# Cross attention of a two-layer decoder: heads in steps of two pairs, with the turned probabilities packed four blocks to a PSUM bank

## The reference

```python
q = (x @ w_q).reshape(B, SQ, 16, 64)       # B = 8, SQ = 112
k = (cond @ w_k).reshape(B, SKV, 16, 64)   # SKV = 375
v = (cond @ w_v).reshape(B, SKV, 16, 64)
attn = softmax(einsum('bqhd,bkhd->bhqk', q, k) * 64 ** -0.5)
out = einsum('bhqk,bkhd->bqhd', attn, v).reshape(B, SQ, 1024)
return out @ w_out + b_out
```

## Time and profile before

| | us |
|---|---|
| three runs | 1166.77, 1177.46, 1171.46 |
| median of them | 1171.46 |
| span of the profiled execution | 1165.0 |
| stage 4's heads in it | from 661.7 to about 961 |

### The profile page before, as it was taken

One profiled execution on the slowest core, in us unless ns is written; L12 is line 12 of the kernel. 1 busy time (PEld: TensorE's weight loads), 2 busy tenths in 40 slices (PEclk: granted clock), 3 DMA queues, 4 the chain that ended last, 5 costly groups with the idle time before them and its releaser, 6 DMA issues.

```text
span 1165.0 us, 21556 instructions
## 1 busy us (share of the span) xinstructions
PE 1001.8 (86%) x8624; PEld 707.4 (61%) x8624; DVE 640.4 (55%) x1519; ACT 588.3 (50%) x1374; POOL 284.6 (24%) x292
## 2 busy tenths in 40 slices
PE   7996898887689988789998799889888897789995
PEld 4664565665388854456655676667666665447654
DVE  3246545666669833454455476776676664527003
ACT  5532565552468844344544354556555544465741
POOL 2521412100500033211112202221132124132733
PEclk9988889898989999899999988999999888679998
DMA  9341464102679785422252243313222105000001
GB/s 311 99 86 40 112 127 110 45 12 98 209 272 314 259 278 168 139 88 85 80 173 88 81 120 105 101 34 107 81 57 78 27 1 226 1 1 1 1 1 32
DMA packets 66676, 123.68 MB, mean 106 GB/s; under 512 B 11632, under 2 KB 41968, under 8 KB 62496
## 3 DMA queue, kind: packets, MB, share of 16 engines
q1 hardware_dynamic: 64528, 117.48, 33.0%
q0 software_dynamic: 2048, 4.82, 1.4%
HBM read 86.30 MB, written 35.92 MB: 105 GB/s over the span
## 4 chain that ended last, share of the span: by engine, by line
PE 56%; DVE 19%; ACT 11%; DMA 5%; issue 4%; POOL 4%; SPq 1%; another core or an unknown queue 0%; DVEq 0%; ACTq 0%; POOLq 0%
PE psum L398 38%; DVE s_p L2695 3%; ACT s_p L2653 3%; POOL rs L2985 2%; PE psum L2612 2%; DVE s_max L2684 2%; PE psum L2623 2%; PE psum L1369 2%; PE psum L2784 1%; DVE s_pT L2676 1%; PE psum L550 1%; DVE s_max L653 1%; PE psum L2173 1%; PE psum L2159 1%; PE psum L2604 1%
## 5 line engine op out<-in xcount | busy, mean ns | idle before, releaser
L2653 ACT ACTIVATE s_p<-psum,s_max 112x375 f32<-112x375 f32 x128 | 72.3, 569 | 87.6 <-DVE s_max L2684 87.6
L693 POOL TENSOR_TENSOR rstd<-meanvar,minus_half 112x1 f32<-112x1 f32 x40 | 23.1, 578 | 279.6 <-DVE meanvar L645 209.9
L653 DVE TENSOR_REDUCE s_max<-psum 112x2 f32<-112x750 f32 x64 | 59.4, 935 | 32.5 <-PE psum L550 31.4
L2985 POOL TENSOR_TENSOR rs<-ms,minus_half 112x32 f32<-112x32 f32 x8 | 43.5, 5442 | 110.3 <-DVE ms L2919 110.3
L398 PE MATMUL psum<-Wv,ctx 128*125 128x512 f16 x240 | 59.6, 392 | 11.2 <-ACT s_v L624 5.4
L398 PE MATMUL psum<-ctx,Wk 128*128 128x375 f16 x320 | 62.8, 331 | 5.0 <-ACT s_yT L2242 2.8
L2684 DVE TENSOR_REDUCE s_max<-psum 112x1 f32<-112x375 f32 x128 | 63.7, 539 | 2.3 <-PE psum L2604 2.1
L2612 PE MATMUL psum<-ident,s_p 112*125 112x112 f32 x384 | 61.4, 294 | 3.9 <-DVE s_p L2695 2.3
L609 ACT ACTIVATE s_k<-psum 128x375 f16<-128x375 f32 x64 | 31.2, 488 | 62.1 <-PE psum L398 59.5
L2604 PE MATMUL psum<-s_k,s_q 64*112 64x375 f16 x384 | 46.0, 345 | 17.0 <-ACT s_p L2653 6.5
L2612 PEld LDWEIGHTS psum<-ident,s_p 112*125 112x125 f32 x384 | 51.7, 198 | 13.7 <-DVE s_p L2695 3.9
(11 more groups left out here) (360 smaller groups left out, 2445.1 us busy)
## 6 DMA issues: line engine op xcount, KB each, us to landing
keys<-s_k SPq DMA_DIRECT2D x64, 187.5 KB, 2.2
s_k<-keys SPq DMA_DIRECT2D x8, 1500.0 KB, 7.6
values<-s_v SPq DMA_DIRECT2D x48, 224.0 KB
s_v<-values SPq DMA_DIRECT2D x16, 672.0 KB
raw_wg<-in_wg SPq DMA_DIRECT2D x8, 1024.0 KB, 6.6
raw_wu<-in_wu SPq DMA_DIRECT2D x8, 1024.0 KB, 7.1
raw_wd<-in_wd SPq DMA_DIRECT2D x8, 1024.0 KB
s_kd<-k_halves SPq DMA_DIRECT2D x48, 93.8 KB, 3.8
```

The source lines that it names most:

```text
L653: VE.tensor_reduce(s1_max[b % 2][:, 2 * p:2 * p + 2], rings["s1"][unit][0:N, :, 0:S], X, ALU.max, negate=True).then_inc(*V.up("max1", n))
L2653: SC.activation(rings["p4"][2 * n + j], rings["s4"][(n, j)][0:N, 0:S], ACT.Exp, bias=s4_max[b % 2][:, h:h + 1], accum_out=s4_sum[b % 2][:, ...
L2985: GP.tensor_tensor(rs5[b % 2][:], ms5[b % 2][:], minus_half[:], ALU.pow).then_inc(*G.up("rs5", b))
```

## The change

Two pairs go together. In step m the stream places the turning of step m-2 (two pairs, twelve blocks, four to a bank in three banks, where it was three to a bank in four), `nm4` of both pairs of step m-1, `sc4` of both pairs of step m, and `av4` of both pairs of step m-2. It yields after each of the three turned banks and after the two `av4`; from the third turned bank to the last `av4` nothing can come between. ACT copies two of the three banks, 448 columns each, DVE the third. `oT4` comes first in its step. There are eight buffers of probabilities instead of six. The planned costs of turning are three times 430 for two pairs, where they were four times 320. Scores, maxima, exps, scalings and products are as they were.

```diff
--- before.py
+++ after.py
@@ -2357,15 +2357,15 @@
         for name, shape in things:
             ffn_w[name] = group.load(ffn_m, name, shape)
             ffn_group[name] = group
+    NS, TURNED = B * HP // 2, 3
     s4_q.append(work.tensor("s4_q1", [P, HP, 2, 2 * N], F16))
     s4_k.append(work.tensor("s4_k1", [P, HP, 2, S], F16))
     s4_v.append(work.tensor("s4_v2", [SCH, NCH, H // 2, DHW]))
-    s4_p = [work.tensor(f"s4_p{i}", [N, S])[:] for i in range(6)]
-    s4_pT = [work.tensor(f"s4_pT{i}", [SCH, NCH * N])[:] for i in range(4)]
+    s4_p = [work.tensor(f"s4_p{i}", [N, S])[:] for i in range(8)]
+    s4_pT = [work.tensor(f"s4_pT{i}", [SCH, TURNED, 4, N]) for i in range(2)]
     s4_max = [work.tensor(f"s4_max{i}", [N, H]) for i in range(2)]
     s4_sum = [work.tensor(f"s4_sum{i}", [N, H]) for i in range(2)]
     assert work.at <= s3_end
-    TO_T, TO_O = 2, 3
     xf = wts.tensor("xf", [P, KC, T_])
     xf16 = wts.tensor("xf16", [P, 2, KC, T_], F16)
     k5 = [wts.tensor(f"k5_{i}", [P, KC, 2, N]) for i in range(2)]
@@ -2391,8 +2391,8 @@
     rings.update(s4=w4, t4=w4, misc4=w4, misc5=w4, o4=banks(6, 1), o5=banks(7, 1),
                  p4=Ring(s4_p), pT4=Ring(s4_pT), sc5=Ring(sc5), pT5=Ring(pT5))
     step("sc4", "T sc4, V maxa4, V maxb4, A expa4, A expb4", cost=500)
-    step("trA4", "T tr4, A pT4", "t4", "A pT4", 320)
-    step("trV4", "T tr4, V pT4", "t4", "V pT4", 320)
+    step("trA4", "T tr4, A pT4", "t4", "A pT4", 430)
+    step("trV4", "T tr4, V pT4", "t4", "V pT4", 430)
     step("nm4", "V +1, V nma4, V nmb4")
     step("av4", "T av4", cost=700)
     step("oT4", "A oT4")
@@ -2459,31 +2459,40 @@
             yield from until(("av4", 4 * (m - 3) + 3))
         yield [("vget", m)]
 
+    def turned_of(h):
+
+        return range(NCH * h // 4, (NCH * h + NCH - 1) // 4 + 1)
+
     def s4_heads():
 
-        for n in range(B * HP + TO_O + 1):
-            b, p = divmod(n, HP)
-            if n < B * HP and p == 0:
-                yield from until(("k4get", b), ("q4", 4 if b > 1 else 3, b - b % 2, HW // P - 1))
-            t, o = n - TO_T, n - TO_O
-            if 0 <= t < B * HP:
-                for h, what in ((2 * t, "trA4"), (2 * t + 1, "trV4")):
-                    rings["pT4"].take(h, (T, ("av4", t)))
-                    place((what, h))
-            if o > 0 and o % 4 == 0:
-                place(("oT4", (o - 1) // HP, (o - 1) % HP // 4))
-            if 0 < n <= B * HP:
-                place(("nm4", n - 1))
-            if n < B * HP:
-                for j, name in enumerate(("expa4", "expb4")):
-                    rings["s4"].take((n, j), (A, (name, n)))
-                    rings["p4"].take(2 * n + j, (T, ("tr4", 2 * n + j)))
-                yield [("sc4", n)]
-            if 0 <= o < B * HP:
-                if o % 4 == 0:
-                    yield from until(("vget", o // 4))
-                    rings["o4"].take(o // 4, (A, ("oT4", o // HP, o % HP // 4)))
-                yield [("av4", o)]
+        for m in range(NS + 3):
+            t = m - 2
+            if t > 0 and t % 2 == 0:
+                place(("oT4", (t - 1) // 4, (t - 1) // 2 % 2))
+            if 0 <= t < NS:
+                rings["pT4"].take(t, (T, ("av4", 2 * t + 1)))
+                for k in range(TURNED):
+                    yield [("trV4" if k == TURNED - 1 else "trA4", t, k)]
+            if 0 < m <= NS:
+                place(("nm4", 2 * m - 2))
+                place(("nm4", 2 * m - 1))
+            if m < NS and m % 4 == 0:
+                yield from until(("k4get", m // 4), ("q4", 4 if m >= 8 else 3, m // 4 - m // 4 % 2, HW // P - 1))
+            if m < NS:
+                for n in (2 * m, 2 * m + 1):
+                    for j, name in enumerate(("expa4", "expb4")):
+                        rings["s4"].take((n, j), (A, (name, n)))
+                        h = 2 * (n % 2) + j
+                        rings["p4"].take(2 * n + j, (T, ("tr4", m, turned_of(h)[-1])))
+                    if n % 2 == 0 or t >= 0:
+                        place(("sc4", n))
+                    else:
+                        yield [("sc4", n)]
+            if 0 <= t < NS:
+                if t % 2 == 0:
+                    yield from until(("vget", t // 2))
+                    rings["o4"].take(t // 2, (A, ("oT4", t // 4, t // 2 % 2)))
+                yield [("av4", 2 * t), ("av4", 2 * t + 1)]
         place(("ffnin",))
 
     def s4_out(b):
@@ -2605,24 +2614,31 @@
                                         k[rows, p, v, :], start=i == 0, stop=i == 2)
                 ins.then_inc(*T.up("sc4", n))
             elif what in ("trA4", "trV4"):
-                h, = at
-                p = rings["p4"][h]
-                pe.wait_ge(V["nmb4" if h % 2 else "nma4", h // 2], *rings["t4"].free(unit))
-                for c in range(NCH):
-                    ins = TE.transpose(rings["t4"][unit][0:SCH, c * N:(c + 1) * N],
-                                       p[:, c * SCH:(c + 1) * SCH], ident[0:N, 0:N])
-                ins.then_inc(*T.up("tr4", h))
+                t, k = at
+                for h in range(4):
+                    if k in turned_of(h):
+                        pe.wait_ge(V["nmb4" if h % 2 else "nma4", 2 * t + h // 2])
+                pe.wait_ge(*rings["t4"].free(unit))
+                for i in range(4):
+                    h, c = divmod(4 * k + i, NCH)
+                    ins = TE.transpose(rings["t4"][unit][0:SCH, i * N:(i + 1) * N],
+                                       rings["p4"][4 * t + h][:, c * SCH:(c + 1) * SCH], ident[0:N, 0:N])
+                ins.then_inc(*T.up("tr4", t, k))
             elif what == "av4":
                 n, = at
                 b, p = divmod(n, HP)
-                pe.wait_ge(A["pT4", 2 * n], V["pT4", 2 * n + 1], L_vget[n // 4 % 3]["vget", n // 4])
+                t = n // 2
+                pe.wait_ge(A["pT4", t, 1], L_vget[n // 4 % 3]["vget", n // 4])
+                if n % 2:
+                    pe.wait_ge(V["pT4", t, TURNED - 1])
                 if p % 4 == 0:
                     pe.wait_ge(*rings["o4"].free(n // 4))
                 for c in range(NCH):
                     for j in range(2):
+                        k, i = divmod(NCH * (2 * (n % 2) + j) + c, 4)
                         ins = TE.matmul(rings["o4"][n // 4][64 * j:64 * j + 64, p % 4 * N:(p % 4 + 1) * N],
                                         s4_v[n // 4 % 3][:, c, 2 * (p % 4) + j, :],
-                                        rings["pT4"][2 * n + j][:, c * N:(c + 1) * N],
+                                        rings["pT4"][t][:, k, i, :],
                                         start=c == 0, stop=c == NCH - 1)
                 ins.then_inc(*T.up("av4", n))
             elif what == "out":
@@ -2640,10 +2656,11 @@
         for unit in plans[4]:
             what, *at = unit
             if what == "trA4":
-                h, = at
-                act.wait_ge(T["tr4", h], *rings["pT4"].free(h))
-                SC.activation(rings["pT4"][h], rings["t4"][unit][0:SCH, 0:NCH * N],
-                              ACT.Copy).then_inc(*A.up("pT4", h))
+                t, k = at
+                act.wait_ge(T["tr4", t, k], *rings["pT4"].free(t))
+                SC.activation(rings["pT4"][t][:, k].rearrange("p i n -> p (i n)"),
+                              rings["t4"][unit][0:SCH, 0:4 * N],
+                              ACT.Copy).then_inc(*A.up("pT4", t, k))
             elif what == "sc4":
                 n, = at
                 b, p = divmod(n, HP)
@@ -2671,10 +2688,10 @@
         for unit in plans[4]:
             what, *at = unit
             if what == "trV4":
-                h, = at
-                dve.wait_ge(T["tr4", h], *rings["pT4"].free(h))
-                VE.tensor_copy(rings["pT4"][h],
-                               rings["t4"][unit][0:SCH, 0:NCH * N]).then_inc(*V.up("pT4", h))
+                t, k = at
+                dve.wait_ge(T["tr4", t, k], *rings["pT4"].free(t))
+                VE.tensor_copy(rings["pT4"][t][:, k].rearrange("p i n -> p (i n)"),
+                               rings["t4"][unit][0:SCH, 0:4 * N]).then_inc(*V.up("pT4", t, k))
             elif what == "sc4":
                 n, = at
                 b, p = divmod(n, HP)
```

## The result

The changed kernel takes 1184.3 us (median of 12 runs) beside 1171.7 for the kernel before: a ratio of 1.0099, with a 95% interval of 1.0066 to 1.0132. Run again beside other kernels it was 1.0068 (1.0032 to 1.0105). It is slower by 0.7 to 1%, where 0.7% faster was forecast.

The account below looks back on a forecast made before the run. TensorE was taken to set the pace, though not alone. Terms -18.8 - 4.4 - 3.0 + 17 + 1 = -8.2 us took 1171.5 to 1163 us; forecast 1155 to 1171 (chance 0.42), range 1147 to 1185.

Parts of the forecast that it names:

- What bounds the kernel: Stage 4: TensorE sets the pace, but not alone; it idles 34.1 of 299 us, partly waiting for exps and copies.
- Part 1: TensorE in stage 4: 125 fewer changes of array split at 0.15 us each, -18.8 us; lower bound 0.09 each, -11.3.
- Part 2: Products' wait for the results' copy (oT4) goes, -4.4 us; clock lost behind it in first 59 us returns, -3.0.
- Part 3: Copies of turned banks: DVE 12.4 us less, ACT 5.6 us more, both hidden by PE's work: 0.
- Part 4: Maxima behind a second scaling on DVE hold banks: 33 us of waits in 31 steps, +17 net of old waits.
- term for s5's waits: Within Part 4: half of PE's 12.2 us of waits for s5's copies and exps, 6 us, taken off the new wait.
- Short of banks: Rival, chance 0.20: steps wait 1.6 us for their second exp, clock gives nothing back, s5 waits stay: +18 us, 1189.
- Waits as they were: Rival, chance 0.22: new wait costs no more than exps did before, both clock episodes go: -28 us, 1143.
- The other half of the chain: Rival, chance 0.10: DVE and ACT hold the pace, a shorter PE list only becomes idle time: 1171, no change.
- The clock: Rival, chance 0.06: new pauses drop TensorE's clock in some eight steps with few fillers: +20 on the sum, 1183.
- What would show it: Stage 4 signs: PE busy 15 to 20 us less, s_p waits some 30, twelve turned blocks 1.5 us, early clock above 0.86.
- signs of being wrong: PE busy falls under 8 us; s_p waits stay 10 or pass 45; or stage length stays while idle replaces work.

Follow-up runs that it names:

- alternating variant: Scalings first, with the first pair's products placed between the two pairs' scores in a step: 1134.0 us, 0.9722 of the kernel before.
- scalings first: The changed kernel with both scalings (nm4) of step m-1 placed first in step m, ahead of the turned banks: 1132.0 us, 0.9716 of the kernel before.
- six copies: Scalings first, plus six DVE copies that nothing needs ahead of each step's maxima: 1203.3 us, 1.0335 of the kernel before.

## Why the prediction was wrong

**What bounds the kernel** was read rightly: PE, held up by banks. All variants move with PE's idle time and clock.

**Part 1, changes of split.** Forecast -18.8 us at 0.15 each. PE's work was 248.6 us before and is 234.8 and 235.0: -13.7, 0.11 us a change, 5 us less than forecast. The price itself is not sharp: 0.12 to 0.13 in the alternating variant, and 0.14 if the kernel before is set against scalings first, which has the changed kernel's list but 3 to 5 us less work. So the value lies between the forecast's bounds of 0.09 and 0.15, and whether the price was too high or waits added to the work is not shown.

**Part 2, the results' copy.** The wait of the products is gone, as forecast (-4.4), but 2.5 us of it came back at the output projection, which also needs the copy. The clock did come back in the first 59 us, 1.00 for 0.86, and was lost again behind it. The changed kernel's first 59 and next 120 us, in its two traces:

```profile
667.00:726.00 59.00, 49.14 (x450) 40.31 (x450) 42.79 (x116) 34.40 (x108) 11.14 (x17) 1.00 0.50 148
726.00:846.00 120.00, 102.61 (x879) 81.44 (x879) 74.62 (x198) 61.55 (x196) 25.41 (x17) 0.91 0.28 78
660.10:719.10 59.00, 49.13 (x450) 40.34 (x450) 42.78 (x116) 34.35 (x107) 11.12 (x17) 1.00 0.50 148
719.10:839.10 120.00, 100.04 (x893) 79.02 (x894) 75.94 (x201) 64.10 (x203) 25.41 (x17) 0.96 0.28 78
```

Where PE was busy for 106.8 of 120 us at full clock it is busy for 102.6 at 0.91 and 100.0 at 0.96: the idle time of this stretch went from 13 us to 17 and 20. Over the whole stage the clock cost 2.5 us more than before in one trace and 2.1 less in the other (half of PE's busy time at 0.50: 16.9 before, 19.4 and 14.8 after), where -3.0 was forecast.

**Part 3, the copies.** The sizes were right: 32 at 623 ns on DVE and 64 at 567 on ACT in the trace after.

```profile
L2661 ACT ACTIVATE s_pT<-psum 125x448 f32<-125x448 f32 x64 | 34.7, 567 | 11.7 <-PE psum L2624 11.4
L2693 DVE COPY s_pT<-psum 125x448 f32<-125x448 f32 x32 | 19.9, 623 | 13.2 <-PE psum L2624 12.9
```

I costed them at nothing; undoing them with the scalings left in their place was not tried. With scalings first they are worth some 18 us. I looked at the share of busy time alone, and neither at the fourth bank nor at what waits for DVE's copy of it.

**Part 4, the new wait, is the step that failed.** Its mechanism was right: a second scaling ahead of the maxima, banks held longer, PE waiting before s5's units and turned blocks. The maxima were forecast 0.95 us later, and the median delay grew by 0.96. The waits for exps were forecast at 33 us and are 29.0. Wrong was what I took off, "some of the 12.2 us for s5, since who waits for the exp finds those ready: half, 6". All other idle time was 23.1 us before, 18.7 without the products' wait for s_attT, and is 23.6 now: plus 5 where -6 was forecast. The exps do not only hold banks. They stand ahead of ACT's other work, and when the maxima are late, so are oT (5.4 us), x_ch (3.5) and s_attT (2.5); with the scalings first these waits are 2.0, 2.2 and 0.7. Nor did the fillers' own work on DVE, 1.4 us ahead of the scalings in the piece above, enter the sum.

In the two traces, stage 4 grew by 7.9 and 3.5 us: work -13.7, idle time +19, clock +2.5 and -2.1. The sum of -8.2 had -18.8, +13.6 (-4.4, +17 and +1) and -3.0. So it misses 5 us in part 1, 5 in the idle time (11 for the other waits, less what the exps fell short) and 1 to 5.5 in the clock, 12 to 16 us together. The term for s5's waits is the largest and the only one with the wrong sign in both traces; the others are mainly wrong in size.

**The rivals.** "Short of banks" (chance 0.20) gives the outcome's sign, and two of its conditions came true: the s5 waits stayed and the clock gave nothing back. Its price did not: its +18 us took 50 us of waits for exps, and they are 29, near the forecast's own 33. "Waits as they were" came true only with the scalings first, which the forecast did not think of moving. "The other half of the chain" described what the stage shows, work shrunk by 14 us and idle time grown by 19, but not the reason: with the scalings first DVE and ACT do the same work in a stage 37 to 44 us shorter, so their order held the pace and not their amount. "The clock" (chance 0.06) expected falls in the steps with few fillers, where the clock was 1.00; it fell behind them. Its sum was 3 us low: it takes off 6.0 for the two old places, of which the forecast's sum already held 3.0, so it gives 1186 and not 1183. Over the kernels the mean clock goes from 0.91 with six copies to 0.99. The Trainium skill (TensorE: Matmul & The Clock Gate, A second HAM failure mode: psum-queue depth-cycling) describes a clock that swings with short pauses from cycling through PSUM's banks; for the whole stretch these traces agree, with 41 and 31 us at 0.50 in the changed kernel, 34 in the kernel before and 7 and 17 with scalings first, though the kernel before's 120 us at 1.00 spoke against it.

**What would show it.** Waits for s_p near 30 us: right. The twelve turned blocks in 1.5 us: 1.56 in the row below. Busy time down by 15 to 20: 11 and 16. A clock above 0.86 in the first part: 1.00, but that said nothing of the rest. Of the signs of being wrong, the last came: the stage did not shrink while idle time grew by more than the work shrank.

```profile
692.08 1.37 PE L2639 MATMUL psum<-s_pT,s_v 125*64 125x112 f32 x24
693.38 1.56 PE L2624 MATMUL psum<-ident,s_p 112*125 112x112 f32 x12
694.96 0.69 PE L2613 MATMUL psum<-s_k,s_q 64*112 64x375 f16 x6
```

## What to carry to other kernels

Grouping work by kind saves changes on TensorE, and doubles what an in-order engine does between one producer and the consumer that frees its banks. Before grouping, list for each shared buffer what stands on every engine from its filling to its release, and move out what does not need the new data: here three moved lines were worth 3.5 to 3.8%, while the grouping without them lost 0.7 to 1%. And follow a late instruction not only to who waits for it, but to what is queued behind it on its own engine.
